# A Fourier-layer tower on one core: three buffers and ScalarE stores in the mixing stage, half-sized input tiles and two group buffers in the inverse stage

## The reference, cut to what matters

```python
h = einsum('bhwi,ic->bhwc', x, fc0_w) + fc0_b; h = h.transpose(0, 3, 1, 2)
for l in range(4):
    xf = rfft2(h)                                   # only 32 x 16 modes are kept
    top = einsum('bixy,ioxy->boxy', xf[:, :, :16, :16], w1[l])    # complex, one 64x64 matrix per mode
    bot = einsum('bixy,ioxy->boxy', xf[:, :, -16:, :16], w2[l])
    sc = irfft2(of)                                 # of holds top and bot, zero elsewhere
    y = sc + einsum('bihw,oi->bohw', h, pw_w[l]) + pw_b[l]
    y = (y - mean(y)) * rsqrt(var(y) + eps) * gamma[l] + beta[l]  # over images and pixels
    h = gelu(y)
```

## Time and profile before

| | us |
|---|---|
| median of three runs (lowest, highest) | 5555.8 (5553.83, 5564.04) |
| the profiled execution | 5561.11 |
| its span on the core | 5559.3 |
| TensorE busy, share of the span | 3813.1, 69% |
| VectorE busy | 2993.7, 54% |
| ScalarE busy | 2535.4, 46% |
| DMA traffic | 1093.16 MB |

### The profile page before, as it was taken

The page is one execution under the profiler, slowest core; times in us unless marked ns, Lnnn a source line. Parts: engine busy times, 40 slices in busy tenths (PEclk is TensorE's granted clock), DMA queues, the critical chain, the costliest instruction groups (busy, mean ns, idle before and its releaser), DMA issues. The chain is left out here.

```text
span 5559.3 us, 115640 instructions
## 1 busy us (share of the span) xinstructions
PE 3813.1 (69%) x50724; PEld 2545.1 (46%) x50724; DVE 2993.7 (54%) x3933; ACT 2535.4 (46%) x1968; POOL 56.9 (1%) x51
## 2 busy tenths in 40 slices
PE   5676885657666656576667566766678994668677
PEld 4354773435455534354555344545552223623532
DVE  1437987853666678536666784366660003344344
ACT  0112335521677755116777451167778991112122
POOL 0000000000000000000000000000000001000000
PEclk9888997888888878888889788888899995579579
DMA  1654656755677667556776675567765431000000
GB/s 34 253 215 172 224 219 258 288 213 226 243 288 289 268 253 289 219 211 257 289 289 257 264 281 224 207 257 288 288 258 206 170 123 36 0 0 1 0 0 8
DMA packets 184510, 1093.16 MB, mean 197 GB/s; under 512 B 20613, under 2 KB 92517, under 8 KB 122465
## 3 DMA queue, kind: packets, MB, share of 16 engines
q1 hardware_dynamic: 160578, 802.32, 37.6%
q10 hardware_dynamic: 22592, 285.22, 13.3%
q0 software_dynamic: 1024, 1.05, 0.1%
HBM read 683.80 MB, written 404.75 MB: 196 GB/s over the span
## 5 line engine op out<-in xcount | busy, mean ns | idle before, releaser
L509 PE MATMUL bank<-arena 128*64 128x128 f32 x16384 | 1130.4, 295 | 161.2 <-ACT arena L552 142.4
L509 PEld LDWEIGHTS bank<-arena 128*64 128x64 f32 x16384 | 1080.0, 221 | 314.0 <-issue 313.9
L587 DVE STREAM_TRANSPOSE arena<-bank 64x512 f32<-64x512 f32 x1024 | 731.4, 714 | 388.2 <-PE bank L485 357.3
L552 ACT ACTIVATE arena<-bank,pwb 128x1024 f32<-128x1024 f32 x512 | 567.0, 1108 | 608.0 <-PE bank L509 603.8
L543 ACT ACTIVATE arena<-arena,shift,scale 64x2048 f32<-64x2048 f32 x384 | 803.0, 2091 | 71.1 <-ACT arena L552 39.4
L361 PE MATMUL bank<-arena 128*32 128x128 f32 x8192 | 596.0, 476 | 309.0 <-DVE arena L388 309.0
L595 DVE BATCH_NORM_STATS2 stats<-arena 128x6 f32<-128x512 f32 x1024 | 634.0, 672 | 228.3 <-ACT arena L552 228.2
L361 PEld LDWEIGHTS bank<-arena 128*32 128x32 f32 x8192 | 423.4, 142 | 481.5 <-issue 327.6
L485 PE MATMUL bank<-arena,ga 64*64 64x512 f32 x2048 | 309.5, 728 | 476.2 <-DMA arena<-spec_out 420.8
L728 ACT ACTIVATE arena<-arena,shift,scale 128x1024 f32<-128x1024 f32 x384 | 445.1, 1230 | 404.5 <-DMA arena<-y_dram 404.3
L688 PE MATMUL bank<-arena,fwq 32*32 32x512 f32 x6144 | 316.9, 842 | 350.5 <-DVE arena L733 350.5
(11 more groups left out here) (208 smaller groups left out, 2845.5 us busy)
## 6 DMA issues: line engine op xcount, KB each, us to landing
arena<-y_dram SPq DMA_DIRECT2D x224, 2048.0 KB, 8.5
y_dram<-arena ACTq DMA_DIRECT2D x128, 2048.0 KB, 8.0
arena<-spec_in SPq DMA_DIRECT2D x32, 2048.0 KB, 8.9
arena<-in_w_modes SPq DMA_DIRECT2D x32, 2048.0 KB, 13.3
spec_out<-arena SPq DMA_DIRECT2D x64, 1024.0 KB, 3.9
arena<-spec_out SPq DMA_DIRECT2D x32, 2048.0 KB, 21.0
spec_in<-arena SPq DMA_DIRECT2D x24, 2048.0 KB, 13.4
spec_in<-arena ACTq DMA_DIRECT2D x4, 4096.0 KB, 11.7
```

The source lines that it names most:

```text
L509: mm = pe.matmul(hpx(bank[4 + T % 2 * 2 + j // 4][CHAN[par], :])[:, :, j % 4 * S:(j % 4 + 1) * S], a2[p % 2][par][:, :, rp], hpx(hin[u][pa ...
L552: act.activation(y, banks[:, 4 + T % 2 * 2:6 + T % 2 * 2, :].rearrange("p b (h x) -> p b h x", h=2), ACT.Identity, bias=pwb[:]).then_inc(y ...
L587: dve.transpose(a2[p % 2][par][FREQ[par], v * 32 + c0:v * 32 + c0 + 16, :], banks[FREQ[par], 2 * v:2 * v + 2, :].rearrange("p r (k c) -> p ...
```

## The change

In mixing, buffers and loops:

```diff
-        w_sb = [at(u * MC * C, MC, C) for u in range(2)]
-        s_sb = [at(2 * MC * C + 2 * u * B * MC, 2, B, MC) for u in range(2)]
+        w_sb = [at(u * MC * C, MC, C) for u in range(3)]
+        s_sb = [at(3 * MC * C + 2 * u * B * MC, 2, B, MC) for u in range(3)]
         def sync_mix(sp, l, first):
+            def load(c):
+                u = c % 3
+                if c > 2:
+                    sp.wait_ge(mix_done, (l * NCH + c) * 2 - 4)
+                sp.dma_start(s_sb[u][:, 0], spec_in[c]).then_inc(s_loaded[u], 16)
+                sp.dma_start(w_sb[u], d["w_modes"][l, c]).then_inc(w_loaded[u], 16)
+            for c in range(3):
+                load(c)
...
+            for c in range(3, NCH):
+                load(c)
```

TensorE's, ScalarE's and VectorE's loops over chunks are written out (8 instead of 4 times 2). What is left out between the first three loads and the others are the small loads of `gamma`, `beta`, `wst` and `pwb`. In what follows `lift` is ScalarE's copy of L376, `rotate` is VectorE's L386 and L388, and what is left out at the end are the four transposes of L394:

```diff
+            lift(0)
+            for c in range(NCH):
+                if c + 1 < NCH:
+                    lift(c + 1)
+                for v in range(2):
+                    act.wait_ge(mixed_turned, (l * NCH + c) * 8 + (4 * v + 12))
+                    act.dma_start(spec_out[2 * c + v], ...).then_inc(mixed_stored[c % 2], 16)

+            rotate(0)
+            for c in range(NCH):
+                if c + 1 < NCH:
+                    rotate(c + 1)
+                dve.wait_ge(mixed_stored[c % 2], ...)
+                for v in range(2):
+                    dve.wait_ge(mix_done, (l * NCH + c) * 2 + (v + 1))
+...
```

In the inverse stage:

```diff
-        yin = [at((6 + u) * PX, PX) for u in range(2)]
+        yin = [at(6 * PX + v * PX // 2, 2, PX // 4) for v in range(2)]
-        grp = at(O1, M2, GI, HB)
+        grp = [at(O1 + v * HB * GI * M2, M2, GI, HB) for v in range(2)]
             def load_group(g):
-                sp.wait_ge(grp_free, l * NG + (g + 1))
+                if g > 1:
+                    sp.wait_ge(grp_free, l * NG + g)
+            def load_half(p, v):
+                if p > 0:
+                    sp.wait_ge(h_ready, (l * NP + p) * 4 + (2 * v - 2))
+                px = slice(v * (ROW2 // 2), (v + 1) * (ROW2 // 2))
+                sp.dma_start(yin[v], hpx(y_dram[p])[:, :, px]).then_inc(in_loaded[v], 16)
             for p in range(NP):
-                if not first:
-                    load_pair(p)
-                if p % Q == 0 and p > 0:
-                    load_group(p // Q)
                 if first:
-                    load_pair(p)
+                    load_x(p)
+                else:
+                    for v in range(2):
+                        load_half(p, v)
+                if p % Q == 0 and p // Q + 1 < NG:
+                    load_group(p // Q + 1)
```

More of the change, by code:

```diff
@@ L288, in gpsimd_spectrum0 @@
             pool.memset(bn[:], 0.0).then_inc(zeroed, 1)
-        w_loaded = [sem("w_loaded_even"), sem("w_loaded_odd")]
-        s_loaded = [sem("s_loaded_even"), sem("s_loaded_odd")]
+        w_loaded = [sem(f"w_loaded{u}") for u in range(3)]
+        s_loaded = [sem(f"s_loaded{u}") for u in range(3)]
         layer_loaded = sem("layer_loaded")
@@ L297, in build, with third @@
         mix_done, mixed_turned = sem("mix_done"), sem("mixed_turned")
-        mix_free, mixed_stored = sem("mix_free"), [sem("mixed_stored_even"), sem("mixed_stored_odd")]
-        w_sb = [at(u * MC * C, MC, C) for u in range(2)]
-        s_sb = [at(2 * MC * C + 2 * u * B * MC, 2, B, MC) for u in range(2)]
+        mixed_stored = [sem("mixed_stored_even"), sem("mixed_stored_odd")]
         HB = C // 2
-        m_sb = [[at(2 * MC * C + 4 * B * MC + (2 * u + v) * B * HB, B, HB) for v in range(2)] for u in range(2)]
-        IT = NCH // 2
-        def sync_mix(sp, l, first):
[L309 to L328, removed]
+        w_sb = [at(u * MC * C, MC, C) for u in range(3)]
+        s_sb = [at(3 * MC * C + 2 * u * B * MC, 2, B, MC) for u in range(3)]
+        m_sb = [[at(3 * MC * C + 6 * B * MC + (2 * u + v) * B * HB, B, HB) for v in range(2)] for u in range(2)]
+        USES = [len(range(u, NCH, 3)) for u in range(3)]
+        def third(l, c):
+            return l * (USES[c % 3] * 16) + (c // 3 * 16 + 16)
+        def sync_mix(sp, l, first):
+            def load(c):
[6 more added lines that the diff above has]
+                load(c)
             for u in range(2):
@@ L340, in sync_mix @@
             for u in range(2):
-                sp.wait_ge(mixed_stored[u], l * (IT * 32) + (IT * 32 + 32))
+                sp.wait_ge(mixed_stored[u], l * (NCH * 16) + (NCH * 16 + 32))
             sp.sem_inc(waited[sp.engine], 1)
         def tensor_mix(pe, l, first):
[L345 to L366, removed]
@@ new lines, in tensor_mix @@
+            for c in range(NCH):
+                u, n = c % 3, l * NCH + c
+                pe.wait_ge(w_loaded[u], third(l, c))
+                pe.wait_ge(real_down, n + 1)
+                pe.wait_ge(imag_up, n + 1)
+                pe.wait_ge(imag_negated, n + 1)
+                for v in range(2):
+                    pe.wait_ge(mixed_turned, n * 8 + (4 * v + 4))
+                    pe.sem_inc(waited[pe.engine], 1)
+                    for k in range(M1):
+                        for t in range(4):
+                            mode = v * K1 + t % 2 * M1 + k
+                            mm = pe.matmul(bank[4 * v + k // 4][t * HB:(t + 1) * HB, k % 4 * 2 * B:(k % 4 + 1) * 2 * B],
+                                           w_sb[u][:, mode, t // 2 * HB:(t // 2 + 1) * HB], s_sb[u][:, :, :, mode],
+                                           start=True, stop=True, tile_position=(0, t * HB))
+                    mm.then_inc(mix_done, 1)
@@ L371, in scalar_mix, with lift @@
                 act.sem_inc(mixed_stored[1], 16 * 2)
[L372 to L376, removed]
+            def lift(c):
+                u = c % 3
+                act.wait_ge(s_loaded[u], third(l, c))
+                act.sem_inc(waited[act.engine], 1)
+                act.activation(s_sb[u][0:C, 1], s_sb[u][C:P, 0], ACT.Copy).then_inc(imag_up, 1)
+            lift(0)
[4 more added lines that the diff above has]
+                    act.wait_ge(mixed_turned, (l * NCH + c) * 8 + (4 * v + 12))
+                    act.sem_inc(waited[act.engine], 1)
+                    act.dma_start(spec_out[2 * c + v], m_sb[c % 2][v].rearrange("p b o -> p (b o)")).then_inc(mixed_stored[c % 2], 16)
         def vector_mix(dve, l, first):
@@ L380, in vector_mix @@
                 dve.sem_inc(mixed_turned, 8)
[L381 to L394, removed]
@@ L399, in build, with rotate @@
-        grp_loaded, grp_free, pair_ready = sem("grp_loaded"), sem("grp_free"), sem("pair_ready")
-        in_loaded = [sem(f"in_loaded{u}") for u in range(2)]
+            def rotate(c):
+                u = c % 3
+                dve.wait_ge(s_loaded[u], third(l, c))
+                dve.sem_inc(waited[dve.engine], 1)
+                dve.tensor_copy(s_sb[u][C:P, 1], s_sb[u][0:C, 0]).then_inc(real_down, 1)
+                dve.wait_ge(imag_up, l * NCH + (c + 1))
+                dve.tensor_scalar(s_sb[u][C:P, 0], s_sb[u][C:P, 0], -1.0, None, ALU.mult).then_inc(imag_negated, 1)
@@ new lines, in vector_mix @@
+            rotate(0)
+            for c in range(NCH):
+                if c + 1 < NCH:
+                    rotate(c + 1)
+                dve.wait_ge(mixed_stored[c % 2], l * (NCH * 16) + (c // 2 * 32 + 32))
+                for v in range(2):
+                    dve.wait_ge(mix_done, (l * NCH + c) * 2 + (v + 1))
+                    modes = banks[:, 4 * v:4 * v + 4, :].rearrange("p q (k r b) -> p b r (q k)", k=4, r=2)
+                    for j in range(4):
+                        dve.transpose(m_sb[c % 2][v][:, 16 * j:16 * j + 16, :], modes[:, 16 * j:16 * j + 16]).then_inc(mixed_turned, 1)
@@ L432, in sync_inverse, with load_x @@
                     sp.sem_inc(y_stored[u], 16)
+                for v in range(2):
+                    sp.sem_inc(in_loaded[v], NP * 16)
             def load_group(g):
-                sp.wait_ge(grp_free, l * NG + (g + 1))
[L435 to L449, removed]
+                if g > 1:
+                    sp.wait_ge(grp_free, l * NG + g)
+                sp.dma_start(grp[g % 2].rearrange("p m b o -> p m (b o)"),
+                             spec_out[:, :, g * (GI * HB):(g + 1) * (GI * HB)].rearrange("m p x -> p m x")).then_inc(grp_loaded[g % 2], 16)
+            def load_half(p, v):
[3 more added lines that the diff above has]
+                sp.dma_start(yin[v], hpx(y_dram[p])[:, :, px]).then_inc(in_loaded[v], 16)
+            def load_x(p):
+                if p > 1:
+                    sp.wait_ge(y_done, p * 4 + 4)
+                for par in range(2):
+                    sp.dma_start(hin[p % 2][par][C * par:C * par + 3, :],
+                                 d["x_pair"][p, 3 * par:3 * par + 3, :]).then_inc(x_loaded[p % 2], 16)
             load_group(0)
@@ L538, in gelu @@
                     return
-                if s % 4 == 0:
-                    act.wait_ge(in_loaded[u], l * (NP // 2 * 16) + (NP // 2 * 16 + p // 2 * 16 + 16))
+                if par == 0:
```

(3 more changed lines are left out.)

13 lines of the change are left out of this document (8 added, 5 removed).

## The result

The changed kernel takes 5235.2 us (median of four, 5232.3 to 5241.2) against 5555.2 before (a fourth run has joined the three of 5555.8): a ratio of 0.942 (0.941 to 0.944), 320 us less. I had said 5093, in a range of 4970 to 5185: the direction was right, the size was not, and the value lies outside the range. The profiled execution's span is 5232.0 us, 327.3 less than before.

What follows compares the result with a forecast made beforehand. Waits, not a full engine, were taken to bound mixing and inverse. Savings of 211 + 13 + 49 + 190 = 463 us, with the median before at 5555.8, gave 5093 us, range 4970 to 5185.

Steps and rivals of the forecast that it cites:

- Mixing, matmuls: Mixing stage: the seven TensorE gaps of 7.54 us go and 18.63 us a chunk stay; 211 us in four layers.
- the slack "for the spectrum": Mixing loads: spectrum lands in 16 us, wanted 21 after issue; the third buffer is covered by these 5 us.
- Mixing, ends and stores: Mixing stage: small loads moved to the front save 13 us; moving the stores alone is worth nothing in bandwidth.
- Inverse, layer 0: Inverse stage, layer 0: the group wait goes, beat 10.18 us; 319 us against 368.2, 49 us less.
- Inverse, layers 1 to 3: Inverse stage: group wait goes, half tiles make the beat 13.4 us; 439 against 502.7, 190 us less in three layers.
- The half lands at ... 10.4 if it starts when the store has landed: Inverse, layers 1 to 3: second half lands 7.2 to 10.4 us after the store's issue; 10.3 taken, 9.7 needed.
- The group in SyncE's queue: Inverse, layers 1 to 3: group load delays half loads by 1.8 to 6.1 us; 4 taken, six times a layer.
- the second, stores ahead of halves and groups: Rival, inverse, layers 1 to 3: beat 13.9 us and 6.1 per group, 5178 us in all; chance 0.15.
- The turn-taking between queues: Inverse loads and stores: each DMA engine alternates queues packet by packet, favouring the stores' long rows over 1 and 4 KB.
- if the beat is above 14, my queueing is: Sign for inverse, layers 1 to 3: a beat above 14 us would show the prediction's queueing wrong.

Runs made afterwards that it cites:

- e2: The changed kernel with each half loaded as one row of 8 KB per partition in place of two rows of 4 KB: 5139.8 us, ratio 0.925.
- e5: The changed kernel with the 2 MB load of a group in four loads of 0.5 MB, spread over three pairs: 5161.9 us, ratio 0.929.

## Why the prediction was right in part and wrong in sum

- **Mixing, matmuls: right.** Gaps gone, 18.4 us a chunk for the 18.63 taken, at 298 GB/s. One reading on the way was wrong: "20 to the us" in the earlier trace rows counts every matmul that a microsecond touches, those under way at its edges too. 256 in 18.63 us are 13.7 to the us; that they are the same at both clocks holds, and only that is used. The two-buffer kernel shows that the slack "for the spectrum" was needed: without it 29 us come back.
- **Mixing, ends and stores: right.** 234 us by the traces against 224, 221 by the medians. The end of a stage gave 4.4 us in layer 1 for the 4 taken. The move of the stores is worth nothing.
- **Inverse, layer 0: mechanism right, size off by 8 us.** I took 10.18 us from beats of the kernel before. VectorE needs 10.69 a pair; before, it caught up during every group wait, so the beats between were shorter than the engine's own work. The new beats have a mean of 10.55.
- **Inverse, layers 1 to 3: here it failed.** The loop was named rightly (the store, then the second half, then its Gelu), and the size of one term was wrong. The failed step is "The half lands at ... 10.4 if it starts when the store has landed", taken as an upper end, with 10.3 put into the sum. Measured are 10.9 us in the beat shown, 11.6 in the mean, and a mean beat of 14.8 for 13.4. In the step's own terms, the store lands after 7.8 us for the 8.0 taken, and the half 3.8 us behind it for 2.4. That is the term that was mis-sized: I priced a half at 434 GB/s, a rate read from a load that was not in the two short rows of `load_half`, and the diff shows those rows. Against 439 us forecast this gives 24 x (14.8 - 13.4) = 34 us a layer. With rows of 8 KB the half still comes 2.8 us behind the store and the beat is 14.0. So e2's 95 us are not the whole miss: some 40 us over the forecast stay there, which the form of the rows does not explain.
- **The group in SyncE's queue: right place, low size.** I took 4 between 1.8 and 6.1, and expected the first half to wait 1 to 6 us; it waits up to 8.3, and the beats are 5.1 us above the others (19.9 against 14.8), or 6 x (19.9 - 17.4) = 15 us a layer over the forecast. The last beat, 9.5 for 13.4, gives 4 back. 34 + 15 - 4 = 45 us a layer, 135 in three. These beats add up to the whole miss; e5, which only cuts the group load in four and spreads it, takes 73 us off.
- **Rivals.** The one that happened is the second, stores ahead of halves and groups, but with a beat of 14.8, beyond its 13.9, and 5.1 a group, within its 6.1; with those it gave 5178. The turn-taking between queues that I named for it from the Trainium skill is not what the beat shown has: there the half's queue moves nothing until the store's 2.10 MB are through. How long a turn is, no run here shows. One sign that I had set, "if the beat is above 14, my queueing is" wrong, came true.
- **The range** reached only to that rival's value. Its beat should have been allowed a transfer as slow as the group load's or slower; I widened the landing and not the rate.

## What to carry to other kernels

A tile without a spare puts the whole latency of its load into the beat, and there every term counts in full: the store ahead, the form of the rows, and, where the load no longer is the last to arrive, each issue on the engine that sets the beat. Before giving up a second input buffer to buy a second buffer for something loaded once in four rounds, try to move that rare load to the front of its queue: it cost three lines here and was worth 137 us more. A price per byte holds only for the row length and layout it was read from, and a beat read between stalls can be shorter than the engine's own work, since the stall lets it catch up.

## What the runs showed of the hardware that I had not expected

The 1 MB load in two rows of 4 KB per partition, 8 KB apart in DRAM, kept the DMA engines 70% busy or more while it moved 209 to 332 GB/s over four microseconds; the same bytes in one row of 8 KB took three, at 205 to 434. Behind the store ahead of it the first landed 3.8 us later, the second 2.8. Two loads of 0.5 MB in neighbouring rows of 4 KB lay between (5205 us, between 5140 and 5235). A load issued 2.5 us behind a 2 MB store on the other queue moved no byte until the store was through, 3.3 us later. And a store's issue on ScalarE, with its wait, left ScalarE idle 0.4 to 0.6 us; two in place of one raised its shortest beat from 12.87 to 13.6 us.
